# Second pass of an edge-gated graph kernel: the turning of messages moved ahead of the product

## What is computed

```
z   = concat(h[src], h[dst], edge) @ W.T + b           # 100000 x 256
z   = batchnorm(z)                                     # statistics over all edges
msg = sigmoid(z[:, :128]) * softplus(z[:, 128:])       # 100000 x 128
out = x + zeros.at[src].add(msg)                       # sums by source node
```

## Time and profile before

| | us |
|---|---|
| median of three runs | 3818.71 |
| the profiled execution | 3811.82 |
| its span, first to last instruction | 3810.0 |
| second pass, first to last indirect write | 2595.9 to 3668.3 |
| sums after it, to the last matmul | 3673.3 to 3793.8 |
| mean granted TensorE clock | 0.836 of 2.4 GHz |

### The profile page before, as it was taken

The page is one execution under the profiler, slowest core; times in us unless marked ns, Lnnn a source line. Parts: engine busy times, 40 slices in busy tenths (PEclk is TensorE's granted clock), DMA queues, the critical chain, the costliest instruction groups (busy, mean ns, idle before and its releaser), DMA issues.

```text
span 3810.0 us, 64994 instructions
## 1 busy us (share of the span) xinstructions
PE 2572.3 (68%) x14952; PEld 1728.3 (45%) x14953; DVE 1875.5 (49%) x4083; ACT 1418.7 (37%) x2638; POOL 2552.8 (67%) x2545
## 2 busy tenths in 40 slices
PE   1788888778888885788888899972212113656348
PEld 1466666645555553344444444431111113555348
DVE  7555655555656566533333333343323234666448
ACT  3333333220000002322222222228877777777700
POOL 4477777467777660477777777755777777777730
PEclk9998999969989897999999999995555556887669
DMA  4233333335545451688888888877665555777358
GB/s 115 67 101 102 101 102 100 122 94 173 180 159 178 161 187 39 205 292 290 285 289 293 285 287 287 290 234 286 217 214 186 196 205 208 269 272 254 113 171 266
DMA packets 339096, 749.99 MB, mean 197 GB/s; under 512 B 66424, under 2 KB 130268, under 8 KB 333856
## 3 DMA queue, kind: packets, MB, share of 16 engines
q1 hardware_dynamic: 242656, 497.83, 37.8%
q0 software_dynamic: 93440, 218.82, 19.3%
q10 hardware_dynamic: 2880, 32.11, 2.2%
HBM read 465.29 MB, written 283.22 MB: 196 GB/s over the span
## 4 chain that ended last, share of the span: by engine, by line
POOL 37%; PE 31%; issue 15%; DVE 7%; DMA 5%; DVEq 3%; ACT 3%; POOLq 0%; SPq 0%; ACTq 0%
POOL m_tab L811 19%; POOL H L780 9%; PE PS L1554 9%; POOL arena L780 8%; PE PS L1564 8%; PE PS L1740 3%; PE PS L1627 2%; PE PS L1550 2%; DMA m_tab<-Q,pos_i 2%; DMA Q<-base_tab 1%; DVEq L1136 1%; PE PS L1609 1%; PE PS L1693 1%; PE PS L1719 1%; DVEq L409 1%
## 5 line engine op out<-in xcount | busy, mean ns | idle before, releaser
L780 POOL DMA_INDIRECT Q<-h_tab,src_i x960 | 954.8, 995 | 405.8 <-issue 273.7
L811 POOL DMA_INDIRECT m_tab<-Q,pos_i x784 | 833.7, 1063 | 275.2 <-issue 234.1
L1749 PE MATMUL PS<-ident,arena 128*128 128x128 f32 x784 | 196.2, 399 | 690.9 <-DVE arena L1452 608.4
L780 POOL DMA_INDIRECT arena<-p_tab,src_i x400 | 381.2, 953 | 262.8 <-DMA p_tab<-arena 141.2
L984 ACT ACTIVATE arena<-PS,LB 128x512 f32<-128x512 f32 x392 | 247.9, 683 | 746.7 <-PE PS L1724 746.7
L1564 PE MATMUL PS<-Q 128*128 x2684 | 420.0, 302 | 147.7 <-DVE Q L1138 65.0
L1749 PEld LDWEIGHTS PS<-ident,arena 128*128 128x128 f32 x784 | 129.0, 200 | 751.1 <-issue 529.0
L1564 PEld LDWEIGHTS PS<-Q 128*128 128x128 f32 x2684 | 355.3, 205 | 234.2 <-issue 229.9
L780 POOL DMA_INDIRECT H<-p_tab,src_i x384 | 363.9, 948 | 117.0 <-issue 116.1
L1724 PE MATMUL PS<-arena,WC 128*128 128x512 f32 x784 | 369.4, 594 | 0.0
L1719 PE MATMUL PS<-H,Q 128*128 x1464 | 352.7, 383 | 0.0
(11 more groups left out here) (231 smaller groups left out, 4351.8 us busy)
## 6 DMA issues: line engine op xcount, KB each, us to landing
z_tab<-arena SPq DMA_DIRECT2D x196, 512.0 KB
Q<-z_tab SPq DMA_DIRECT2D x196, 512.0 KB, 6.0
Q<-m_tab SPq DMA_DIRECT2D x234, 264.0 KB, 3.8
arena<-in_edge_t SPq DMA_DIRECT2D x196, 256.0 KB, 3.3
m_tab<-arena SPq DMA_DIRECT2D x48, 792.0 KB
m_tab<-src_i SPq DMA_DIRECT2D x112, 264.0 KB
arena<-dst_tab SPq DMA_DIRECT2D x196, 128.0 KB, 4.1
count_tab<-Q SPq DMA_DIRECT2D x11, 1568.0 KB
```

What stands on the lines that cost most here:

```text
L780: nc.gpsimd.indirect_dma_start(row(s, k), None, table, bass.IndirectOffsetOnAxis(src_i[:, t:t + 1], 0)).then_inc(landed[s], 16)
L811: nc.gpsimd.indirect_dma_start(m_tab, bass.IndirectOffsetOnAxis(pos_i[:, t:t + 1], 0), mrow[:, s, k, :], None).then_inc(ms.scattered[s], 16)
L1749: ins = turn(PS[:, 2 + q, t * P:(t + 1) * P], msg_t[:, q, t * P:(t + 1) * P], ident[:])
```

## The change

PE now turns the gate and the two terms of softplus separately, before the product; the second term is added to the first in PSUM by an ordinary matmul with the identity (no transpose mode). DVE copies the turned gate out of PSUM, multiplies it with the turned softplus in PSUM and writes the rows. ScalarE makes max(z, 0) by Relu. `take_rows`, `scale_z` and `soften` go. The turned softplus has banks 0 and 1, the turned gate banks 2 and 3.

```diff
# ScalarE
 def gates(d, s):
     act.wait_ge(ms.z_in[s], eight_of(d) * 16 + 16)
-    act.wait_ge(ms.msg_t_ready, group_of(d, s) + 1)
+    act.wait_ge(ms.turned, group_of(d, s) + 1)
+def positive(d, s):
+    nc.scalar.activation(core[s], zin[:, s, GE:2 * GE], ACT.Relu, bias=bn[:, 11:12], scale=bn[:, 9:10]
+                         ).then_inc(ms.relu_ready, 1)
-def take_rows(d, s):
-    act.wait_ge(ms.turned, g + 3)
-    if not (isinstance(d, int) and d == 0):
-        act.wait_ge(ms.scattered[s], eight_of(d) * (16 * GT))
-    nc.scalar.copy(mrow[:, s, :, 0:F], PS[:, 2 + q, :].rearrange("p (a b) -> p a b", b=F))
-    nc.scalar.copy(mrow[:, s, :, F:F + 1]..., columns(src_f, g)).then_inc(ms.row_ready, 1)
 def pass2(d, s):
     if s % SL == 0:
-        four(d, s, gates); rows(0); four(d, s, size); rows(1)
-        four(d, s, small_power); rows(2); four(d, s, logarithm); rows(3)
+        for stage in (gates, size, positive, small_power, logarithm):
+            four(d, s, stage)
# VectorE
 def message(d, s):
-    dve.wait_ge(ms.soft_ready, g + 1)
-    dve.wait_ge(ms.turned, g + 1)
-    v.tensor_tensor(msg_t[:, q, :], gate[:, s, :], soft[:, s, :], ALU.mult).then_inc(ms.msg_t_ready, 1)
+    dve.wait_ge(ms.turned, g + (RZ + 1))
+    if not (isinstance(d, int) and d == 0):
+        dve.wait_ge(ms.scattered[s], eight_of(d) * (16 * GT))
+    v.tensor_copy(gate_rows[:, q, :], PS[:, 2 + q, :]).then_inc(ms.gate_taken, 1)
+    dve.wait_ge(ms.gate_taken, g + 1)
+    v.tensor_tensor(mrow[:, s, :, 0:F], PS[:, q, :]..., gate_rows[:, q, :]..., ALU.mult)
+    v.tensor_copy(mrow[:, s, :, F:F + 1]..., columns(src_f, g)).then_inc(ms.row_ready, 1)
 def pass2(d, s):
-    for n, stage in ((1, soften), (2, message)):
-        at = back8(d, s, n)
-        if at:
-            stage(*at)
+    at = back8(d, s, 2)
+    if at:
+        message(*at)
     if back8(d, s, 0):
         for k, o in sorted_of(d, s):
             sum_sorted(k, o)
-    at = back8(d, s, -AHEAD)
-    if at:
-        scale_z(*at)
# TensorE
-def turn_msg(d, s):
-    pe.wait_ge(ms.msg_t_ready, g + (RZ + 1))
+def turn_parts(d, s):
+    pe.wait_ge(ms.relu_ready, g + (RZ + 1))
     pe.wait_ge(ms.row_ready, g + 1)
     for t in range(GT):
-        ins = turn(PS[:, 2 + q, t * P:(t + 1) * P], msg_t[:, q, t * P:(t + 1) * P], ident[:])
+        turn(PS[:, 2 + q, t * P:(t + 1) * P], gate[:, s, t * P:(t + 1) * P], ident[:])
+    for t in range(GT):
+        mm(PS[:, q, t * P:(t + 1) * P], core[s][:, t * P:(t + 1) * P], ident[:], is_transpose=True,
+           start=t == 0, stop=False, skip_group_check=True)
+    pe.wait_ge(ms.ln_ready, g + 1)
+    for t in range(GT):
+        ins = mm(PS[:, q, t * P:(t + 1) * P], soft[:, s, t * P:(t + 1) * P], ident[:],
+                 start=False, stop=True, skip_group_check=True)
     ins.then_inc(ms.turned, 1)
```

More of the change, by code:

```diff
@@ L47, in build_gnn @@
     MR = 10
-    LAG, AHEAD = 10, 4
+    LAG = 10
     PER = 2 * MR
@@ L271, in build_gnn @@
         soft, a = carve(arena, a, RZ, GE)
-        msg_t, a = carve(arena, a, 2, GE)
+        gate_rows, a = carve(arena, a, 2, GE)
         outs, _ = carve(q_space, 0, 3, NB * F)
@@ L384, in build_gnn @@
         ms = Sems()
-        ms.z_in, ms.act_step, ms.dve_step = ring("msg_z_in", RZ), sem("msg_act_step"), sem("msg_dve_step")
-        ms.abs_ready, ms.ln_ready, ms.soft_ready = sem("msg_abs_ready"), sem("msg_ln_ready"), sem("msg_soft_ready")
-        ms.msg_t_ready, ms.turned = sem("msg_t_ready"), sem("msg_turned")
+        ms.z_in, ms.act_step, ms.relu_ready = ring("msg_z_in", RZ), sem("msg_act_step"), sem("msg_relu_ready")
+        ms.abs_ready, ms.ln_ready = sem("msg_abs_ready"), sem("msg_ln_ready")
+        ms.gate_taken, ms.turned = sem("msg_gate_taken"), sem("msg_turned")
         ms.row_ready, ms.scattered, ms.pads_zeroed = (
@@ L718, in pass2 @@
                     g = group_of(*at)
-                    sp.wait_ge(ms.dve_step, g + 1)
+                    sp.wait_ge(ms.relu_ready, g + 1)
                     sp.wait_ge(ms.abs_ready, g + 1)
@@ L1014, in logarithm @@
                 nc.scalar.activation(soft[:, s, :], soft[:, s, :], ACT.Ln, bias=1.0).then_inc(ms.ln_ready, 1)
-            def take_rows(d, s):
-                g, q = group_of(d, s), s % 2
-                act.wait_ge(ms.turned, g + 3)
-                if not (isinstance(d, int) and d == 0):
-                    act.wait_ge(ms.scattered[s], eight_of(d) * (16 * GT))
-                nc.scalar.copy(mrow[:, s, :, 0:F], PS[:, 2 + q, :].rearrange("p (a b) -> p a b", b=F))
-                nc.scalar.copy(mrow[:, s, :, F:F + 1].rearrange("p a b -> p (a b)"), columns(src_f, g)
-                               ).then_inc(ms.row_ready, 1)
             def four(d, s, stage):
@@ L1031, in pass2 @@
             def pass2(d, s):
-                def rows(n):
-                    at = back8(d, s + n, SL)
-                    if at:
-                        take_rows(*at)
                 if s % SL == 0:
[L1037 to L1044, removed]
+                    for stage in (gates, size, positive, small_power, logarithm):
+                        four(d, s, stage)
             act.wait_ge(norm.ready, 1)
-            act.wait_ge(ms.pads_zeroed, 1)
-            act.sem_inc(ms.row_ready, 2)
+            act.sem_inc(ms.relu_ready, RZ)
             act.sem_inc(ms.abs_ready, RZ)
-            in_eights(act, SL, pass2)
+            in_eights(act, 0, pass2)
         @block.vector
@@ L1432, in sum_sorted @@
                     add_sum(k * PER + (base + o - SD + 1), (o + 1) % SD)
[L1434 to L1445, removed]
             def message(d, s):
                 g, q = group_of(d, s), s % 2
-                dve.wait_ge(ms.soft_ready, g + 1)
-                dve.wait_ge(ms.turned, g + 1)
-                v.tensor_tensor(msg_t[:, q, :], gate[:, s, :], soft[:, s, :], ALU.mult).then_inc(ms.msg_t_ready, 1)
-            def pass2(d, s):
-                if isinstance(d, int) and (d, s) == (0, 0):
-                    for n in range(AHEAD):
-                        scale_z(0, n)
-                for n, stage in ((1, soften), (2, message)):
-                    at = back8(d, s, n)
-                    if at:
-                        stage(*at)
+                dve.wait_ge(ms.turned, g + (RZ + 1))
[3 more added lines that the diff above has]
+                dve.wait_ge(ms.gate_taken, g + 1)
+                v.tensor_tensor(mrow[:, s, :, 0:F], PS[:, q, :].rearrange("p (a b) -> p a b", b=F),
+                                gate_rows[:, q, :].rearrange("p (a b) -> p a b", b=F), ALU.mult)
+                v.tensor_copy(mrow[:, s, :, F:F + 1].rearrange("p a b -> p (a b)"), columns(src_f, g)
+                              ).then_inc(ms.row_ready, 1)
+            def pass2(d, s):
+                at = back8(d, s, 2)
+                if at:
+                    message(*at)
                 if back8(d, s, 0):
@@ L1464, in pass2 @@
                         sum_sorted(k, o)
-                at = back8(d, s, -AHEAD)
-                if at:
-                    scale_z(*at)
             dve.wait_ge(norm.ready, 1)
-            dve.sem_inc(ms.msg_t_ready, RZ)
-            dve.sem_inc(ms.dve_step, RZ)
+            dve.wait_ge(ms.pads_zeroed, 1)
+            dve.sem_inc(ms.row_ready, 2)
             dve.wait_ge(sg.sums_zeroed, 1)
@@ L1754, in pass2 @@
                 if at:
-                    turn_msg(*at)
+                    turn_parts(*at)
                 if back8(d, s, 0):
@@ L1760, in _ @@
             pe.wait_ge(norm.ready, 1)
-            pe.sem_inc(ms.turned, 2)
+            pe.sem_inc(ms.turned, RZ)
             in_eights(pe, 2, pass2)
```

## The result

The changed kernel took 3828.18 us (median of 20 runs, 3814.8 to 3837.19), the kernel before 3815.20 (median of 20 runs by then, 3808.82 to 3823.70). The ratio is 1.0031, 95% interval 1.0022 to 1.0039: 13 us slower. The forecast was 3883, 64 us slower, range 3812 to 3966. The direction was right and the size was not: the measured loss is a fifth of it.

A forecast was written before the change was run, and what follows sets the result against it. POOL bounds the kernel before; in the 64 steps with sums a closed PE-DVE chain of 7.6 us takes over, ending the pass at 3732 instead of 3668.3: +64 on the 3818.7 median gives 3883 us, range 3812 to 3966.

The forecast's parts named there:

- POOL as the bound and its floor: Second pass: POOL's indirect writes at 1.27 us each, 784 of them, make 996 of 1072 us.
- DVE instructions that read PSUM leave POOL alone: Second pass: DVE products of two SBUF tensors lengthen POOL's writes, PSUM reads do not; 38 + 3 us go.
- The small copy: DVE's copy of 4 columns per group, 0.19 us: about 3 us of longer writes, left out of the sum.
- The leftover of the one-hots: Stretch with sums: one-hot products keep SBUF inputs, so about 15 of 34 us of longer writes would stay.
- ScalarE and the start hidden: Second pass: ScalarE's 17.0 us per four groups hides behind POOL's 20.3; first write within 1 us of before.
- The ring: 64 steps with sums: turning, message, one-hot, sums form a closed chain, 6.6 us at 2.4 GHz, 10.4 at 1.2.
- I take a little above the row, 0.82: Mean clock assumed for the 64 steps, from the kernel before's 0.79 there: 64% of the time at full clock.
- 7.6 us per step: Length of each of the 64 steps with sums at the assumed clock, against 5.08 for POOL's four writes; 486 us.
- Rival 3: 64 steps with sums: closed chain at full clock, 6.6 us per step, 422 us; +0, 3819 us; chance 8%.
- Rival 1: 64 steps with sums: DVE and PE overlap, POOL stays the bound; -60, 3759 us; chance 7%.
- Rival 2: 64 steps with sums: transposes idle for the clock, which falls to 0.65; 8.9 us steps, +147, 3966; chance 18%.
- the forecast's own range: Whole kernel: 3845 us (clock 0.91, 7.0 us steps) to 3935 (clock 0.70, 8.4 us steps); forecast's chance 67%.

The follow-up runs named there:

- the one-hots first: Changed kernel with DVE making a step's one-hots before the message, so they run while PE turns: 3755.56 us, ratio to the kernel before 0.9851.
- the pairs with spare products: One-hots made before the message, plus two spare DVE products per group: ratios 1.0288, 1.0231, 1.0189 with SBUF inputs; 1.0329, 1.0272, 1.0263 with one in PSUM.
- PE kept busy on the slowed chip: Changed kernel with two gate copies and 12 idle-time identity turns per step, where the kernel before took 4386 to 4446 us: 4647.81 us, ratio 1.0459.

## Why the prediction was partly right

- **POOL as the bound and its floor**: right. The 448th write was put near 3164 and started at 3160.3 in the changed kernel, 3163.3 with the one-hots first. Counted from the first write it came 569.6 us later, for 447 x 1.27 = 568; the longer writes went away, 37 us.
- **DVE instructions that read PSUM leave POOL alone**: right, by the changed kernel's trace and the pairs with spare products. The small copy was put at 3 us; before the sums all longer writes together are about 1.
- **The leftover of the one-hots**: put at 15 us, measured 22 in the changed kernel and 21 with the one-hots first. The share of the instructions, 160 of 350, left out that the one-hots fall on other starts now: in this stretch 83 longer writes started under one, in the kernel before 61 of 127.
- **ScalarE and the start hidden**: right; ScalarE waits for turns in the steps, and the first write comes 33.1 us after the last statistic (L1403 before, L1387 after) in both.
- **The ring**: right in every link and in its length at the full clock: 6.6 put, 5.99 and 6.89 measured, 6.44 on average. At 1.2 GHz it was put at 10.4; no step ran whole at that clock. POOL's groups in hand lasted some 20 steps and not ten, since both the steps (6.80, not 7.6) and POOL's groups there (5.4, not 5.08) were other than put.
- **The step that failed**: "I take a little above the row, 0.82". The row was that of the kernel before, 0.79, whose PE, behind a first wait of 16 us, worked in bursts with 4.5 to 8.9 us of idleness between them. The ring has another rhythm, 2.2 us idle in each step, and its clock was 0.94. That the ring stays closed was right; the clock granted in it was carried over from the wrong stretch without a reason. The term "7.6 us per step" measured 6.80; 64 x 0.8 = 51 us is the whole of the error of 51 (64 forecast, 13 measured); that it comes out to the microsecond is luck, as the smaller errors above cancel. Rival 3, the ring at full clock, "+0" at 8%, was the nearest: with 14 of 63 steps 1.6 us longer, 22 us, less the 0.16 by which the average full-clock step was under 6.6, 10 us, it gives +12. Neither it nor the forecast had this mixture.
- **Rival 1** (-60, the ring doesn't close) was wrong for this kernel and is what the one-hots-first version did: 3759 put, 3755.56 measured.
- **Rival 2** (turns are idle for the clock): wrong. But a lower clock in such a ring exists: one more copy of 0.69 us brought it to 0.80 and the time to 3933.
- **The range** 3812 to 3966 held the time, but the forecast's own range, 3845 to 3935, did not: it let the clock go from 0.70 to 0.91 and not above, though the first pass stood in the rows at 1.00.

## What to carry to other kernels

When an engine's reads are moved behind another engine's work, draw what each has in program order for one step and look for a closed chain; if there is one, its length, not the busy shares, is the step. Here putting one call before another made a kernel that lost 0.3% into one that wins 1.5%. And never carry a mean clock over from a stretch with another rhythm: work the ring out at both clocks, and ask how long the array idles in one turn.

## What the runs showed of the hardware that was not expected

- The mean clock changed steeply with the ring's idle stretch. With 1.5 us of it per step (gate copied beside the turns) it was 0.99, with 2.2 us 0.94, with 2.8 us 0.80; a step took 5.74, 6.80 and 8.45 us. An instruction of 0.69 us in the ring cost 1.65, one taken out gave 1.06. PE's busy share changed along with the idle stretch (74, 68 and 67%), and the runs don't tell the two apart; with PE kept busy on the slowed chip the idle stretch was 1.5 us in most steps with two sums and about 3 in most with three, and the clock 0.91.
- Transposes alone had a mean clock of 0.75 where they and matmuls together had 0.74.
- An indirect write of POOL became longer when it started under a DVE product of two SBUF tensors (80 of 84), and not under the same product with one input in PSUM (0 of 79).
- A copy of 128x512 from PSUM on DVE took 0.69 us, the same as a product with a PSUM input.
